# Small expert units: the next unit's front first, keys split on VectorE, weights issued by ScalarE, output rows stored last

## The reference, cut to what matters

```
logits = x @ router_w + router_b;  probs = softmax(logits);  top2 = top_k(probs, 2)
for e in range(4):                         # per batch
    xg = the tokens that have e in top2    # 200 to 800 of 1024 here
    q, k, v = xg @ wq[e] + bq[e], xg @ wk[e] + bk[e], xg @ wv[e] + bv[e]
    att = softmax(q k^T * 0.5, over the valid tokens)      # 16 heads of 16
    y = (att v) @ wo[e] + bo[e]
    out[those tokens] += probs[..., e] * y
```

## Time and profile before

| | us |
|---|---|
| median of 3 runs | 4718.21 |
| lowest and highest | 4715.30, 4719.28 |
| the profiled execution | 4689.79 |
| its span | 4688.0 |
| mean granted clock of TensorE | 0.882 of full speed |

### The profile page before, as it was taken

How to read it: one execution, slowest core, us unless ns; L and a number is a source line. 1 busy time by engine, 2 the same in 40 slices (tenths; PEclk the granted TensorE clock), 3 DMA queues, 4 the chain that set the end, 5 groups by cost and what they waited for, 6 DMA issues and landing times.

```text
span 4688.0 us, 57467 instructions
## 1 busy us (share of the span) xinstructions
PE 3590.1 (77%) x20509; PEld 1616.1 (34%) x20510; DVE 2428.9 (52%) x5520; ACT 2103.1 (45%) x4546; POOL 926.6 (20%) x686
## 2 busy tenths in 40 slices
PE   3988998486687866888767877679278868788795
PEld 1344443323332322323233332323123424234574
DVE  3666665361273612736226452254376787875523
ACT  1656556154355543464444634337145535453121
POOL 1132322300110002100021000200243323100174
PEclk8999999688899988998888978889688979899897
DMA  5444443411421213312143121420432414113288
GB/s 140 148 140 139 138 134 108 128 36 56 118 66 37 56 55 100 77 31 61 46 112 75 28 70 39 109 65 21 123 87 82 119 43 118 40 50 97 79 197 227
DMA packets 326590, 421.39 MB, mean 90 GB/s; under 512 B 43997, under 2 KB 283045, under 8 KB 316679
## 3 DMA queue, kind: packets, MB, share of 16 engines
q1 hardware_dynamic: 302228, 373.50, 28.1%
q0 software_dynamic: 18432, 35.67, 3.4%
q10 hardware_dynamic: 5248, 4.79, 0.3%
HBM read 240.32 MB, written 164.04 MB: 86 GB/s over the span
## 4 chain that ended last, share of the span: by engine, by line
PE 48%; DVE 24%; ACT 6%; issue 6%; DMA 6%; SPq 4%; PEldq 2%; POOL 2%; ACTq 1%; PEld 0%; POOLq 0%; DVEq 0%; another core or an unknown queue 0%
PE PSUM L725 12%; PE PSUM L703 9%; PE PSUM L688 8%; DVE M L946 8%; PE PSUM L634 6%; DVE M L949 5%; ACT P L886 3%; DVE PSUM L952 3%; PE PSUM L747 2%; PE PSUM L566 2%; SPq L1388 2%; DVE best L1279 2%; DVE XR L1282 1%; PE PSUM L670 1%; DMA qk_d<-PH 1%
## 5 line engine op out<-in xcount | busy, mean ns | idle before, releaser
L886 ACT ACTIVATE P<-PSUM 128x512 f32<-128x512 f32 (+2 forms) x3520 | 1557.9, 504 | 860.5 <-PE PSUM L703 531.9
L688 PE MATMUL PSUM<-KS,QS 99*128 99x512 bf16 (+3 forms) x3520 | 933.1, 356 | 472.9 <-SPq L1839 265.3
L946 DVE TENSOR_REDUCE M<-PSUM 128x1 f32<-128x896 f32 (+3 forms) x960 | 938.4, 1023 | 659.4 <-PE PSUM L688 655.1
L703 PE MATMUL PSUM<-QS,KS 101*128 101x512 bf16 (+2 forms) x3520 | 1068.9, 347 | 141.4 <-ACT P L886 94.6
L725 PE MATMUL PSUM<-P,VA 128*17 128x512 f32 (+3 forms) x7040 | 800.9, 527 | 8.8 <-ACT P L886 8.8
L949 DVE TENSOR_REDUCE M<-PSUM 128x1 f32<-128x640 f32 (+6 forms) x704 | 584.9, 831 | 173.7 <-PE PSUM L688 170.2
L703 PEld LDWEIGHTS PSUM<-QS,KS 101*128 101x128 bf16 x3520 | 328.6, 100 | 997.2 <-ACT P L886 601.7
L617 POOL TENSOR_TENSOR QF<-QF,PH 128x1024 f32<-128x1024 f32 (+1 forms) x98 | 174.7, 1783 | 2338.3 <-ACT PH L850 2285.7
L688 PEld LDWEIGHTS PSUM<-KS,QS 99*128 99x128 bf16 x3520 | 297.3, 102 | 928.1 <-SPq L1839 271.3
L952 DVE CUSTOM_DVE_ANT_0 PSUM<-PSUM,mask 128x128 f32<-128x128 f32 x1024 | 284.6, 301 | 250.8 <-PE PSUM L688 250.8
L634 PE MATMUL PSUM<-XT,W 128*128 128x512 f32 x656 | 342.8, 652 | 17.8 <-issue 10.8
(11 more groups left out here) (189 smaller groups left out, 3293.4 us busy)
## 6 DMA issues: line engine op xcount, KB each, us to landing
qk_d<-PH SPq DMA_DIRECT2D x192, 256.0 KB
xg_d<-GX SPq DMA_DIRECT2D x19, 1152.0 KB, 11.3
yg_d<-GX SPq DMA_DIRECT2D x17, 1152.0 KB, 8.5
QS<-qk_d SPq DMA_DIRECT2D x48, 384.0 KB, 5.7
KS<-qk_d SPq DMA_DIRECT2D x48, 384.0 KB, 6.1
XF<-xg_d SPq DMA_DIRECT2D x18, 1024.0 KB, 7.2
VA<-n_L_ffn_expert_gate_up_w SPq DMA_DIRECT2D x64, 256.0 KB, 3.5
qk_d<-PH SPq DMA_DIRECT2D x108, 128.0 KB
```

Of the source, the lines that this page charges most:

```text
L688: mm = e.matmul(slot_heads(s, hb)[:, x, a:b], QS[0:KA, g, h + x, 128 * qt:128 * qt + 128], KS[0:KA, g, h + x, a:b], start=True, stop=True)
L703: mm = e.matmul(s[:, 0:q1 - q0], KS[0:KB, g, j, 128 * kt:128 * kt + 128], QS[0:KB, g, j, q0:q1], start=True, stop=not diag, skip_group_che ...
L886: e.activation(P[:, m % NP, 0:q1 - q0], s[:, 0:q1 - q0], ACT.Exp, scale=ly.scale).then_inc(S["act_p"], 1)
L946: e.tensor_reduce(m[:, 0, qt, h:h + hb], v[:, :, 0:kn], AX.X, ALU.max).then_inc(S["dve_a"], 1)
```

## The change

Five things. (1) For units of at most SMALL = 3 tiles unit_order lays the first passes of all four groups end to end, the first half of the next unit's qp, spl and qs behind group 1, the second half ahead of the second passes (behind group 3 where the next unit is of one piece, in the second pass of group 1 where it has two), and then the four second passes. The next rows' transposes come right behind the value projections, at the front. (2) In these units spl of the keys (w=1) is VectorE's; that of the queries stays GpSimd's. (3) Where the next unit is of 4 tiles or less, its second half uses columns 512 on of QF and PH, and waits for no store. (4) nx and wo are issued by ScalarE instead of SyncE, in units of every size. (5) yo is placed behind every other task of the unit. In the order of tasks (1) and (5) come to this for the sizes that occur: the lists for 6 and 7 tiles are the same as before; for 2 tiles, before and after (numbers: group, or unit and index; x4: four tasks):

```diff
+SMALL = 3
...
+    def vector_split(self, ix):
+
+        if self.layer.name == "moe":
+            return self.layer.nt <= SMALL and ix[1:2] == (1,)
+        return self.first_keys(ix)
+
     def split(self, *ix):
 
-        return ("dve_x" if self.first_keys(ix) else "pool_s", "spl") + ix
+        return ("dve_x" if self.vector_split(ix) else "pool_s", "spl") + ix
+
+    def half(self, i, g2):
+
+        return 512 * g2 if self.layer.name == "moe" and self.layer.of(i).n == 512 else 0
...
-    step, alone, rows = 0.84 * nt * nt, 0.6 * nt * nt, 8.0
-    first = [(0.0, alone / 0.82)] + [(alone + step * g, step) for g in range(3)]
-    second = []
-    for g in range(4):
-        t = first[g][0] + 0.82 * first[g][1] + rows
-        second.append((max(t, second[-1][0] + step) if second else t, step))
+    step, small = 0.84 * nt * nt, nt <= SMALL
+    if small:
+        alone = 0.6 * nt * nt
+        first = [(alone * g + (3.0 if g > 1 else 0.0), 1.22 * alone) for g in range(4)]
+        second = [(4 * alone + 6.0 + max(step, 3.4) * g, max(step, 3.4)) for g in range(4)]
+    else:
+        alone = 0.6 * nt * nt
+        first = [(0.0, alone / 0.82)] + [(alone + step * g, step) for g in range(3)]
+        second = []
+        for g in range(4):
+            t = first[g][0] + 0.82 * first[g][1] + 8.0
+            second.append((max(t, second[-1][0] + step) if second else t, step))
     ev += attention_steps(layer, 1, first, second)
...
+    if small:
+        ev += [(0.1 + 0.1 * k, ("vp", 1, c, h)) for k, (c, h) in enumerate(layer.pairs())]
+        ev += [(second[0][0] + 1.0, ("bv", 1)), (second[0][0] + 2.0, ("bb", 1))]
+        x = 0.5
+    else:
+        ev += [(1.0 + 2.0 * k, ("vp", 1, c, h)) for k, (c, h) in enumerate(layer.pairs())]
+        ev += [(first[1][0] + 2.0, ("bv", 1)), (first[1][0] + 4.0, ("bb", 1))]
+        x = 1.0 + 2.0 * len(layer.pairs())
+    ev.append((x, ("nv", 2)))
+    for c in range(layer.next.nch):
+        ev += [(x + (0.2 if small else 1.5) * c + (0.1 if small else 0.75) * k, ("xt", 2, c, k)) for k in range(2)]
+    ev.append((x + 3.0, ("nr", 3)))
+    for g2 in range(2):
+        if small:
+            y = 2 * alone + 0.5 if g2 == 0 else second[0][0] - 2.0 if layer.next.nch == 1 else second[1][0]
+            d = 0.3
+        else:
+            y = x + 3.5 if g2 == 0 else max(x + 23.5, second[1][0])
+            d = 2.5 if g2 == 0 or step < 20.0 else 6.0
+        for w in range(2):
+            for c in range(layer.next.nch):
+                ev.append((y, ("qp", 2, w, g2, c)))
+                y += d
+            if small:
+                ev += [(y + 0.7, ("spl", 2, w, g2)), (y + 2.0, ("qs", 2, w, g2))]
+            else:
+                ev += [(y - 1.0, ("spl", 2, w, g2)), (y + 6.0, ("qs", 2, w, g2))]
...
-    ev.append((t + 2.8, ("yo", 1)))
...
+    ev.append((max(t for t, task in ev) + 1.0, ("yo", 1)))
...
-            name, n = O.split(i, wi, g2)[0], O.layer.of(i).n
-            f, hi, mid, lo = QF[:, wi, 0:n], PH[:, wi, 0, 0:n], PH[:, wi, 1, 0:n], PH[:, wi, 2, 0:n]
+            name, a = O.split(i, wi, g2)[0], O.half(i, g2)
+            b = a + O.layer.of(i).n
+            f, hi, mid, lo = QF[:, wi, a:b], PH[:, wi, 0, a:b], PH[:, wi, 1, a:b], PH[:, wi, 2, a:b]
             done = O.at(name, *task)
             if O.layer.name == "l1":
                 w.wait_ge("act_x", "rh", i, wi, g2)
             else:
                 w.wait_ge("act_a", "qp", i, wi, g2, O.layer.of(i).nch - 1)
-            if g2 == 1:
+            if g2 == 1 and a == 0:
                 w.wait_ge(f"qst{wi}0", "qs", i, wi, 0)
-            else:
+            elif g2 == 0:
                 w.wait_ge(f"qst{wi}1", "qs", i - 1, wi, 1)
...
+        def next_weights(e, v):
+
+            for k, nm in enumerate(("wq", "wk")):
+                e.dma_start(W[:, k, :, :], kn_weights(d["L0_ffn_" + nm][row(v["nex"]), :, :].rearrange(
+                    "o a b -> (o a) b"))).then_inc(S["next_in"], 16)
+            for k, nm in enumerate(("bq", "bk")):
+                e.dma_start(bq[:, k, :], d["L0_ffn_" + nm][row(v["nex"]), :].rearrange(
+                    "o (g p) -> p (o g)", p=128), allow_slow_non_contiguous=True).then_inc(S["next_in"], 16)
+
+        def output_weights(e, v):
+
+            e.dma_start(W[:, 3, :, :], kn_weights(d["L0_ffn_wo"][row(v["ex"]), :, :].rearrange(
+                "o a b -> (o a) b"))).then_inc(S["wo_in"], 16)
+            e.dma_start(BOB[:, :], d["L0_ffn_bo"][row(v["ex"]), :].to_broadcast([128, C])).then_inc(S["wo_in"], 16)
+            e.dma_start(BVC[:, :], d["L0_ffn_bv"][row(v["ex"]), :].rearrange("o (g p) -> p (o g)", p=128),
+                        allow_slow_non_contiguous=True).then_inc(S["wo_in"], 16)
...
+                elif kind == "nx" and moe:
+                    next_weights(e, v)
+                elif kind == "wo":
+                    output_weights(e, v)
...
-                elif kind == "spl" and O.first_keys(task[1:]):
+                elif kind == "spl" and O.vector_split(task[1:]):
```

More of the change, by code:

```diff
@@ new lines, in unit_order @@
+    ev += attention_steps(layer, 1, first, second)
+    ev += [(-1.0 + 0.1 * w + 0.05 * g, ("ql", 1, w, 2 + g)) for w in range(2) for g in range(2)]
+    ev += [(-0.7, ("mk", 1, 1)), (-0.6, ("nx", 2)), (-0.5, ("wo", 1))]
+    if small:
[6 more added lines that the diff above has]
+        x = 1.0 + 2.0 * len(layer.pairs())
@@ L400, in unit_order @@
     end = second[1][0] + step
+    ev += [(max(end - step * (1 - g), x + 21.5) + 0.1 * w + 0.2 * g, ("ql", 2, w, g)) for w in range(2) for g in range(2)]
+    ev.append((max(end, x + 21.5) + 0.3, ("mk", 2, 0)))
     for c in range(layer.nch):
@@ L404, in unit_order @@
         ev += [(t + 2.0 + 0.5 * h, ("op", 1, c, h)) for h in range(2) if layer.pair(c, h)]
-    ev.append((t + 2.8, ("yo", 1)))
[L406 to L417, removed]
-    ev += [(max(end - step * (1 - g), x + 18.0) + 0.1 * w + 0.2 * g, ("ql", 2, w, g)) for w in range(2) for g in range(2)]
-    ev.append((max(end, x + 18.0) + 0.3, ("mk", 2, 0)))
+    ev.append((max(t for t, task in ev) + 1.0, ("yo", 1)))
     order = Order(layer)
@@ L834, in attention_act @@
                     _, _, wi, g2, c = task
-                    if g2 == 1:
+                    if g2 == 1 and O.half(i, g2) == 0:
                         w.wait_ge(*O.split(i, wi, 0))
@@ L844, in attention_act @@
                     m = ly.wide(c)
-                    x, a = s[:, 0:m], 512 * c
+                    x, a = s[:, 0:m], 512 * c + O.half(i, g2)
                     if l1:
@@ L1316, in attention_pool @@
                     e.tensor_tensor(QF[:, wi, :], QF[:, wi, :], QSW[:, :], ALU.add).then_inc(S["pool_r"], 1)
-                elif kind == "spl" and not O.first_keys(task[1:]):
+                elif kind == "spl" and not O.vector_split(task[1:]):
                     split(e, w, O, task)
@@ L1365, in attention_sp @@
                     for g in (2 * g2, 2 * g2 + 1):
-                        w.wait_ge(f"qld{wi}{g}", "ql", i - 1, wi, g)
+                        if moe and g < 2:
+                            w.carried(f"ahead_ld{wi}{g}", 48)
+                        else:
+                            w.wait_ge(f"qld{wi}{g}", "ql", i - 1, wi, g)
                     done = S[f"qst{wi}{g2}"]
@@ L1493, in attention_sp @@
                     e.dma_start(XF[:, :, :], x_rows(1)).then_inc(S["x_in"], 16)
-                elif kind == "nx":
-                    if l0:
-                        w.wait_ge("act_a", "qp", i - 1, 1, 1, 1)
-                    for k, nm in enumerate(("wq", "wk")):
-                        e.dma_start(W[:, k, :, :], kn_weights(d["L0_ffn_" + nm][row(v["nex"]), :, :].rearrange(
-                            "o a b -> (o a) b"))).then_inc(S["next_in"], 16)
-                    for k, nm in enumerate(("bq", "bk")):
-                        e.dma_start(bq[:, k, :], d["L0_ffn_" + nm][row(v["nex"]), :].rearrange(
-                            "o (g p) -> p (o g)", p=128), allow_slow_non_contiguous=True).then_inc(S["next_in"], 16)
+                elif kind == "nx" and l0:
+                    w.wait_ge("act_a", "qp", i - 1, 1, 1, 1)
+                    next_weights(e, v)
                 elif kind == "nv":
```

21 lines of the change are left out of this document (6 added, 15 removed).

## The result

The changed kernel takes 4757.66 us (median of 4 runs, 4751.84 to 4762.81) against 4716.76 (4 runs, 4710.57 to 4719.28) beside it: a ratio of **1.0088, 95% interval 1.0071 to 1.0106**. It is slower, by twice what I forecast. The profiled execution took 4751.84 us with a span of 4750.0.

A forecast was written before the change was run, and what follows sets the result against it. No one engine was taken as the limit, so the 16 expert units were priced: +69 - 35 - 15 = +19 us, about 4738 on the median. The forecast's own range was 4728 to 4764, the whole range 4686 to 4785.

The forecast's parts named there:

- Part 1: 3-tile units, new order and key split on VectorE: 91 us against 73.7, 17 longer each, +69 for four units.
- the ceiling of +23: Upper bound on the growth of a 3-tile unit, in us, with a slow clock.
- four in a row at 1.72 us: 3-tile unit, first half of the projections: 1.72 us each on TensorE, last copy ending at T 28.8.
- rival (b): Slower still: a lower clock in 3-tile units costs 6 to 8 us more each, +30 in all, about 4768; chance 0.17.
- the sign that I had named: 3-tile unit's granted clock under 0.9 would make the forecast fall the other way.
- Part 2: 2-tile units: work -3 and gap -5.7 sum to -9 us each (bounds -4 and -13), -35 for four.
- The step about the gap: After a 2-tile unit, key stores out earlier: 12.0 instead of 17.7 us to the next unit, -5.7.
- 57 against 60.1: 2-tile unit's work in us, forecast against the kernel before: -3.
- Part 3: Weights issued by ScalarE in all 16 units: first projection of large units no longer waits, -15 us, range 0 to -22.
- Rival (a): Faster: phases apart run freely, 3-tile units grow by under 12.5 us; at +3 each, about 4680; chance 0.24.
- Rival (c): No change: gains and losses cancel, 3-tile units at +10 to +15 us; chance 0.13.
- The contention term: VectorE's split beside GpSimd's in all eight small units: 5.1 us, 3.2 without; sum some 12 us lower without the rule.

The follow-up runs named there:

- e9: Changed kernel; in 3-tile units, scores of groups 2 and 3 issued twice, one of group 2 ten times: 4782.59 us, ratio 1.0149 to the kernel before.
- e6: Changed kernel with both splits of small units, queries and keys, on VectorE: 4744.71 us, ratio 1.0068 to the kernel before.
- e8: Changed kernel with the small units' value bias steps placed before the second half's projections: 4744.18 us, ratio 1.0077 to the kernel before.
- e3: Changed kernel with every split of the units on GpSimd again: 4694.02 us, ratio 0.9996 to the kernel before.
- e2: Kernel before with nx and wo issued by ScalarE, and first-half stores waiting on the carried semaphore: 4654.33 us, ratio 0.9910 to the kernel before.
- e1: Changed kernel with SMALL = 2, so 3-tile units take the old branch again: 4652.3 us, ratio 0.9911 to the kernel before.
- e4: Changed kernel; 3-tile units' first-half projections spread among the scores of groups 1 and 2: 4737.63 us, ratio 1.0077 to the kernel before.
- e10: Changed kernel with SMALL = 2, all unit splits on GpSimd and the value bias steps early: 4651.42 us, ratio 0.9852 to the kernel before.

## Why the prediction was right, and where it was not

The direction and its mechanism were right, the sizes of all three terms were off.

**Part 1, the 3-tile unit: +17 forecast, +21.4 measured** (within the ceiling of +23). The walk against the trace of the first unit, T from its first matmul at 1196.82: second maximum T 7.9 (8.3 forecast, though from a row that I misread: T 5.2 in the earlier trace rows is the third maximum, the second stood at T 1.8, so the opening lost more than the 3 us I added); row of group 1 out 20.6 (20.3); last copy 31.6 (28.8); end of the split 36.8 (34), 5.2 us long where 5.1 was taken; first exponential 52.6 (48.6); end of the groups 88.1 (84.5), so the second pass was 35.5 us where I had 35.9; to the store another 8.0 (6.5). What failed is the step "four in a row at 1.72 us": they took 9.80 us together, the first ones slow, and the output projection took 4.38 us where it had been 2.86. Both are the clock of rival (b). I had that rival apart, at 0.17, as if either it or the forecast would hold; both did. The granted clock fell below 0.9, the sign that I had named, but the price inside the unit was some 4 us and not 6 to 8, because most of the slow stretch lies where VectorE sets the pace (12.9 us against 12.7, under e9). The Trainium skill (TensorE: Matmul & The Clock Gate, Part 1) tells of a clock halved after idling, and the windows agree with it: 0.50 behind 2.98 us of work in ten.

**Part 2, the 2-tile unit: -9 forecast, -1.3 measured.** The step about the gap held: -4.6 where -5.7 was forecast. The step that failed is "57 against 60.1": work was 63.9. Three things were left out. The key split is on the path twice there, and its cast of 0.43 us takes 1.26 beside GpSimd (e6). The value bias stands behind it (e8, 2.0 us on the mean and some 3 at an equal clock). And three of the four units ran at 0.70 to 0.73 where before they had 0.73 to 0.82; about 5 to 6 us separate the same unit at 0.70 to 0.73 and at 0.83. The first two are the larger part: with the split off VectorE the unit takes 58.3 to 58.4, near my 57, and does so at a clock of 0.72 to 0.76, so 5.5 of the 6.9 us go with the split. What the new order itself does there is seen in e3 against e2, both with the weights on ScalarE: work 58.4 against 57.2, gap 12.6 against 18.2. The phases apart cost 1.2 us, some of which may be the clock (0.72 to 0.75 in e3, 0.74 to 0.82 in e2), and the stores that no longer trail give back 5.6.

**Part 3, the weights: -15 forecast, -31 after, -43 alone (e2).** I had bounds of 0 and -22, and the trace is outside. The mis-sized term is the wait of 2.81 and 1.38 us: I took part of it, for fear that VectorE bounds the group anyway, when in truth all of it came back, and with it the slow matmuls behind it (4.35 us in place of 2.81 in the first 6-tile unit, more in the later ones). In the 2-tile unit a term was missing altogether: the wait of 2.6 to 3.1 us for the value bias's load, put at nothing, of which e2 got 2.3 us back.

**The sum.** +69 - 35 - 15 = +19 was forecast; measured +86 - 5 - 31 = +50 in the profiled units, +41 in the medians. Errors of +17 and +30 were partly cancelled by one of -16; the total is in the forecast's own range (4728 to 4764) partly by that luck, the terms are not what I made them. Rival (a), the pass of gaps that costs less than it seemed, is excluded by e1 and e3: 72 us in the old branch, 90 in the new order with the best placing of the split. Rival (c) fell with the ratio.

The contention term was right in size: the split took 5.2 us (5.1 forecast), and e3 gives back 5.5. But costing it as contention missed the larger point, that **any** work of VectorE there stands between the projections and the maxima: 3.1 us of it would remain without a meeting (e6), and GpSimd did the job without delaying the unit.

## What to carry to other kernels

Two passes that use different engines for their results (VectorE's maxima, ScalarE's exponentials) are worth overlapping where the unit is full: laid end to end they cost 16 to 17 us of 74 here where TensorE was 84% busy, and 1.2 us of 57 where it was 67% busy, less than the earlier stores gave back. Work that only the next stage needs belongs on the engine that nobody waits for, even if it is slower there (5.4 us against 3.1 for a split of 1024 columns here). And DMA issues moved off a queue of twenty to an engine that is idle at that moment gave more than the wait they removed, because the matmuls behind the wait were slow as well.

## What the runs showed of the hardware

- VectorE's subtraction of two SBUF operands started at 1228.49 beside GpSimd's instruction of 1228.47 to 1230.59 and ended at 1231.67: 1.08 us behind that one's end, where it needs 1.22 alone. The two times read as a step that stood nearly still until the other was done. A close of 0.17 us with two SBUF inputs did the same in e4: begun at 1219.25, ended at 1220.42, with GpSimd's instruction ending at 1220.39. The Trainium skill (SBUF — State Buffer, Who interferes with whom) calls the shared ports an exclusive lock, and both rows agree. So even a small VectorE step costs what is left of GpSimd's instruction, 1.1 us for the close and 2.1 for the subtraction here, which I had not expected for steps as small as a close.
- A cast with one SBUF input was held as well (1260 ns against 426), at 512 columns; at 1024 columns it met no GpSimd instruction and took 693. GpSimd lost time in these meetings as well: its last instruction of a split of 512 columns took 1.48 us beside VectorE's cast and 1.16 in e3, where VectorE had no split.
- The clock of units with the same instructions in the same execution came out as 0.83 or 0.70, for 59.8 or 65.5 us (after), and as 0.87 or 0.72, for 53.0 or 59.2 (e10). In a kernel with such units a difference of 1 to 2 us a unit can't be told from where the clock happened to fall, unless units of equal clock are compared.
